# Squared lengths in 64-row tiles, and a new order of work between the two halves of a four-block network kernel

## The reference, cut to what matters

```python
# X is (8, 512, 128); every block is x = x + block(layernorm(x))
P = X @ W_in + b_in                      # 16 heads, each with Q, K, V, G of 64
d2 = q2[:, None] + k2[None, :] - 2*qk    # q2, k2: squared lengths of rows of Q, K
W  = (1e-4 + sqrt(max(d2, 0))) ** -2
W  = W / (1e-4 + sum(W, -1))
out1 = (G * (W @ V)) @ W_out + b_out
# block 2: 8 experts, top 2 of a softmax: sum_e r_e * (relu(x W1_e + b1_e) W2_e + b2_e)
# block 3: linear attention with decay;  block 4: 384 of 512 tokens go through gelu(x W)
```

## Time and profile before

| | us |
|---|---|
| median of 3 runs | 1470.9 (1470.77 to 1471.15) |
| the profiled execution | 1468.7 |
| its span, first to last instruction | 1466.6 |
| TensorE busy in the span | 1403.2 |
| ScalarE busy | 1098.1 |
| VectorE busy | 1059.6 |
| GpSimd busy | 851.9 |
| mean granted TensorE clock | 0.981 of 2.4 GHz |

### The profile page before, as it was taken

The page is one execution under the profiler, slowest core; times in us unless marked ns, Lnnn a source line. Parts: engine busy times, 40 slices in busy tenths (PEclk is TensorE's granted clock), DMA queues, the critical chain, the costliest instruction groups (busy, mean ns, idle before and its releaser), DMA issues.

```text
span 1466.6 us, 17689 instructions
## 1 busy us (share of the span) xinstructions
PE 1403.2 (96%) x6304; PEld 718.6 (49%) x6304; DVE 1059.6 (72%) x1944; ACT 1098.1 (75%) x943; POOL 851.9 (58%) x667
## 2 busy tenths in 40 slices
PE   6999999999999999999999999699999999999974
PEld 3433434434433443443444343256777777777753
DVE  6786777777777777777777677654677687786674
ACT  2799789879978978978878879845676676676741
POOL 4568767777777678768867876721333333333320
PEclk9999999999999999999999999899999999999985
DMA  3001111011001002001101103333011011010100
GB/s 114 0 16 23 30 30 24 15 45 23 16 16 51 16 16 51 16 17 30 37 16 30 30 16 96 89 123 103 0 66 58 8 66 55 11 66 8 59 7 8
DMA packets 45847, 55.09 MB, mean 38 GB/s; under 512 B 13825, under 2 KB 32513, under 8 KB 44609
## 3 DMA queue, kind: packets, MB, share of 16 engines
q1 hardware_dynamic: 45760, 53.97, 12.3%
HBM read 49.11 MB, written 4.85 MB: 37 GB/s over the span
## 4 chain that ended last, share of the span: by engine, by line
PE 89%; DVE 7%; POOL 1%; ACT 1%; issue 1%; DMA 0%; SPq 0%; DVEq 0%; POOLq 0%
PE sc L383 16%; PE av L396 14%; PE pj L74 13%; PE z L74 12%; PE y L1095 8%; PE sc L378 6%; PE y L74 5%; PE pj L362 4%; PE pj L412 4%; PE pj L404 2%; DVE w L541 2%; PE tb L1026 1%; POOL wsum L303 1%; PE tb L1040 1%; PE tb L1053 1%
## 5 line engine op out<-in xcount | busy, mean ns | idle before, releaser
L541 DVE TENSOR_SCALAR w<-sc 128x1024 f32<-128x1024 f32 x256 | 301.3, 1218 | 117.3 <-PE sc L383 115.2
L632 ACT ACTIVATE w<-w 128x2048 f32<-128x2048 f32 x128 | 237.5, 1904 | 144.5 <-DVE w L541 144.2
L303 POOL TENSOR_TENSOR wsum<-wsum,w 128x512 f32<-128x512 f32 x256 | 329.0, 1285 | 20.1
L882 POOL TENSOR_TENSOR hr_l<-hr,hr_h 128x512 fp32r<-128x512 f32 x112 | 150.2, 1341 | 265.0 <-ACT hr L928 265.0
L383 PE MATMUL sc<-query,key 64*128 64x512 f32 x1024 | 254.4, 615 | 0.0
L396 PE MATMUL av<-w,vt 128*64 128x512 f32 x1024 | 237.6, 607 | 6.4 <-DVE gT L548 5.2
L636 ACT ACTIVATE w<-w 128x2048 f32<-128x2048 f32 x128 | 240.2, 1901 | 0.4
L640 ACT ACTIVATE w<-w 128x2048 f32<-128x2048 f32 x128 | 239.6, 1895 | 0.0
L928 ACT ACTIVATE hr<-z,b 128x512 f32<-128x512 f32 x256 | 173.7, 684 | 77.3 <-PE z L74 77.2
L289 POOL TENSOR_TENSOR sqq<-query 128x512 f32<-128x512 f32 x64 | 66.5, 1040 | 223.0 <-DVE query L495 220.9
L300 POOL TENSOR_TENSOR wsum<-w 128x512 f32<-128x512 f32 x128 | 164.5, 1285 | 11.5 <-ACT w L640 11.5
(11 more groups left out here) (183 smaller groups left out, 2237.6 us busy)
## 6 DMA issues: line engine op xcount, KB each, us to landing
hT<-head_recips SPq DMA_DIRECT2D x64, 256.0 KB, 4.0
rb<-routing SPq DMA_DIRECT2D x8, 2048.0 KB, 7.0
w<-in_W SPq DMA_DIRECT2D x16, 256.0 KB, 5.0
xa<-in_X SPq DMA_DIRECT2D x8, 256.0 KB, 4.4
xc<-in_X SPq DMA_DIRECT2D x8, 256.0 KB, 2.8
x<-xc SPq DMA_DIRECT2D x8, 256.0 KB, 4.0
out<-prod SPq DMA_DIRECT2D x8, 256.0 KB, 2.3
x<-x SPq DMA_DIRECT2D x1, 1792.0 KB, 10.9
```

Of the source, the lines that this page charges most:

```text
L303: nc.gpsimd.tensor_tensor(wsum[:, u, :], wsum[:, u, :], w[:, j % 2, u, c, :], ALU.add).then_inc(s_added, 1)
L541: nc.vector.tensor_scalar(w[:, s, 2 * r:2 * r + 2, c, :], sc[:, i, :, :], 0.0, None, ALU.max).then_inc(s_d2, 1)
L632: nc.scalar.activation(w[:, j % 2, u, :, :], w[:, j % 2, u, :, :], ACT.Sqrt).then_inc(s_sqrt, 1)
```

## The change

1. **Rows in 64-row tiles.** `qrow` and `krow` hold head v of a pair at partitions 64v. `qrow` holds both pairs r of a quad in different rows of the same 64 (r = 0 at rows 0 to 3, r = 1 at rows 32 to 35), and `krow` gets one copy per pair, [P, 2, 2, T], which is zero in the other pair's rows. So L378 contracts over 64 rows, in the tiles of L383. The key rows take four VectorE instructions instead of two (`key_rows`: high and all, for r = 0 and 1, on one `high` tile), the query rows still two. `row_factors` in the prologue grows from 5 to 8 tiny instructions.
2. `nsel` and its load, and the tile `xn`, go: the layernorm writes in place, so `xa`'s next load waits for the transposes and stands after normalizer(j) of q = 2 instead of q = 1.
3. **Last quad's sums.** GpSimd no longer adds the chunks of quad 31; `last_sums` multiplies ones with all four chunks on TensorE, 16 fp32 products instead of 4.
4. **Order between the halves.** On all engines, as in the diff. ScalarE mixes the first relus among the last logarithms and powers; root_f(0) goes before the square roots.
5. Waits for the tail's loads, for `ones2`, for `w2s` and `x1_out` move to their first use.

```diff
-                        u = 2 * (g % 2) + v
-                        nc.tensor.matmul(sc[:, i, v, :], krow[32 * u:32 * u + 32, j % 2, c * P:(c + 1) * P],
-                                         qrow[32 * u:32 * u + 32, j % 2, :], start=True, stop=False)
+                        nc.tensor.matmul(sc[:, i, v, :], krow[halves[v], j % 2, g % 2, c * P:(c + 1) * P],
+                                         qrow[halves[v], j % 2, :], start=True, stop=False)
...
+            def last_sums():
+
+                n = bank(("sum", NQ - 1))
+                pe.wait_ge(s_w, 4 * NQ)
+                for c in range(NC):
+                    for u in range(4):
+                        m = nc.tensor.matmul(pj[32 * u:32 * u + 32, n, :], ones[:, :], w[:, (NQ - 1) % 2, u, c, :],
+                                             start=(c == 0), stop=(c == NC - 1))
                 m.then_inc(s_pj, 1)
...
+            def key_rows(j):
+                dve.wait_ge(s_pj_free, use["q2", j] + 1)
+                source = pj[:, bank(("k2", j)), :]
+                for r in range(2):
+                    if r == 1:
+                        dve.wait_ge(s_high, 4 * j + 3)
+                    high_rows(source, row_any[:, r, 1:2], row_one[:, r, 0:1])
+                    dve.wait_ge(s_high, 4 * j + 2 * r + 2)
+                    nc.vector.scalar_tensor_tensor(krow[:, j % 2, r, :], source, row[:, r, 3:4], high[:, :].bitcast(F32),
+                                                   ALU.mult, ALU.subtract).then_inc((s_high, s_pj_free)[r], 1)
...
-            sp.wait_ge(att["added"], 12 * NQ)
+            sp.wait_ge(att["pj"], use["sum", NQ - 1] + 1)
...
             square_roots, logarithm, power = att_scalar(act)
+            root_f(0)
             square_roots(NQ - 1)
-            root_f(0)
             nc.scalar.preload_act_table_set("natural_log_exp_and_others")
             logarithm(NQ - 1, 0)
-            for u in range(4):
-                if u < 3:
-                    logarithm(NQ - 1, u + 1)
-                if u == 3:
-                    exponential(0)
-                power(NQ - 1, u)
+            logarithm(NQ - 1, 1)
+            power(NQ - 1, 0)
+            power(NQ - 1, 1)
+            exponential(0)
+            logarithm(NQ - 1, 2)
             act.wait_ge(S["in_front"], 16 * len(front_loads))
+            hidden(0)
+            hidden(1)
+            power(NQ - 1, 2)
+            hidden(2)
+            hidden(3)
+            logarithm(NQ - 1, 3)
+            hidden(4)
+            power(NQ - 1, 3)
+            hidden(5)
+            turned_routing(0)
...
-                if (b, k) == (0, 0):
-                    sums(NQ - 1)
+                if (b, k) == (0, 1):
+                    turn_routing(0)
                 if (b, k) == (0, 2):
+                    weighted_values(NQ - 1, 1)
+                if (b, k) == (0, 3):
+                    last_sums()
+                if (b, k) == (0, 7):
                     output(NQ - 2)
-                if (b, k) == (0, 14):
+                if (b, k) == (0, 16):
                     output(NQ - 1)
-                if (b, k) == (0, 16):
+                if (b, k) == (0, 18):
                     turn_output(B - 1)
...
+            turn_f(0)
             pe.wait_ge(S["in_front"], 16 * len(front_loads))
-            turn_f(0)
             logits(0)
-            weighted_values(NQ - 1, 0)
-            weighted_values(NQ - 1, 1)
             for n in range(AHEAD):
                 if n == 2:
-                    turn_routing(0)
+                    weighted_values(NQ - 1, 0)
                 hidden(n)
...
-                if (b, k) == (0, 5):
+                if (b, k) == (0, 4):
+                    weighted_values(NQ - 1, 1)
                     sums(NQ - 1)
-                if (b, k) == (0, 6):
+                    for e in range(5, NE):
+                        split_w1(e)
+                if (b, k) == (0, 8):
                     output(NQ - 2)
-                if (b, k) == (0, 8):
                     dve.wait_ge(S["in_b2"], 16)
-                    dve.wait_ge(att["added"], 12 * NQ)
-                if (b, k) == (0, 9):
+                if (b, k) == (0, 12):
                     reciprocals(NQ - 1)
-                if (b, k) == (0, 19):
+                if (b, k) == (0, 20):
                     output(NQ - 1)
...
+            dve.wait_ge(att["added"], 12 * (NQ - 1))
+            front_norm(0)
             sums(NQ - 2)
             output(NQ - 3)
-            dve.wait_ge(att["added"], 12 * (NQ - 1))
-            front_norm(0)
-            split_w1(0)
             dve.wait_ge(S["turn_f"], 1)
             V.tensor_copy(xT_f[:, :], front_bank(0)).then_inc(S["xT_f"], 1)
             hand_over(0)
+            split_w1(0)
             dve.wait_ge(S["in_front"], 16 * len(front_loads))
             softmax_start(0)
-            reciprocals(NQ - 2)
-            for e in range(1, 4):
-                split_w1(e)
-            weighted_values(NQ - 1, 0)
+            split_w1(1)
             softmax_end(0)
             expert_ranks(0)
             routing(0)
-            for e in range(4, NE):
-                split_w1(e)
-            weighted_values(NQ - 1, 1)
+            weighted_values(NQ - 1, 0)
+            split_w1(2)
+            reciprocals(NQ - 2)
+            split_w1(3)
+            split_w1(4)
```

More of the change, by code:

```diff
@@ L110, in build_attention @@
         qrow = sb("qrow", [P, 2, T], F32R)
-        krow = sb("krow", [P, 2, T], F32R)
-        high = sb("high", [P, 2, T], F32R)
-        nsel = sb("nsel", [P, 2, P])
+        krow = sb("krow", [P, 2, 2, T], F32R)
+        high = sb("high", [P, T], F32R)
         head = sb("head", [P, 2, 32])
[L115 to L118, removed]
+        row = sb("row", [P, 2, 4])
+        row_one = sb("row_one", [P, 2, 2])
+        row_any = sb("row_any", [P, 2, 2])
+        both_one = sb("both_one", [P, 2])
+        both_any = sb("both_any", [P, 2])
+        row_low = sb("row_low", [P, 1])
         stats = sb("stats", [P, NC, 6])
@@ L244, in sync @@
             load_x(xc, 0, s_xc)
-            sp.wait_ge(s_xn, NC)
+            sp.wait_ge(s_pj, use["turn", 0, 1] + 1)
             load_x(xa, 1, s_xa)
@@ L271, in sync @@
                     load_x(xc, b, s_xc)
-                if q == 1 and b + 2 < B:
-                    sp.wait_ge(s_xn, NC * (b + 2))
+                if q == 2 and b + 2 < B:
+                    sp.wait_ge(s_pj, use["turn", b + 1, 1] + 1)
                     load_x(xa, b + 2, s_xa)
@@ L310, in normalize @@
                                         gT[:, 2 * q:2 * q + 2, :], ALU.mult).then_inc(s_hT, 1)
-            for j in PERIODS:
+            for j in range(-1, NQ):
                 if 0 <= j - 3 < NQ:
@@ L324, in gpsimd @@
                         add_chunks(j - 1, u)
+            return normalize
         def tensor(pe):
@@ L459, in tensor @@
                     step(j, k)
-            return weighted_values, sums, output, turn_output
+            return weighted_values, sums, last_sums, output, turn_output
         def vector(dve):
@@ L510, in row_factors @@
[L510 to L518, removed]
@@ L520, in high_rows @@
-            def high_rows(j, name):
-                h, out, factor, one, low = rows[name]
-                nc.vector.tensor_scalar(high[:, h, :], pj[:, bank((name, j)), :], factor, one,
-                                        ALU.mult, ALU.add).then_inc(s_high, 1)
-            def all_rows(j, name):
-                h, out, factor, one, low = rows[name]
-                dve.wait_ge(s_high, 2 * j + h + 1)
+                nc.vector.tensor_tensor(row_one[:, :, :], row[:, :, 0:4:2], row[:, :, 1:4:2], ALU.subtract).then_inc(s_row, 1)
@@ new lines, in row_factors, with high_rows, query_rows @@
+                nc.vector.tensor_scalar(row_low[:, :], row_low[:, :], 0.25, None, ALU.mult).then_inc(s_row, 1)
+                dve.wait_ge(s_row, 7)
+                nc.vector.tensor_scalar(both_any[:, :], both_any[:, :], 0.25, None, ALU.mult).then_inc(s_row, 1)
+                dve.wait_ge(s_row, 8)
+            def high_rows(source, factor, one):
+                nc.vector.tensor_scalar(high[:, :], source, factor, one, ALU.mult, ALU.add).then_inc(s_high, 1)
+            def query_rows(j):
+                if j >= 1:
+                    dve.wait_ge(s_pj_free, use["k2", j - 1] + 1)
+                source = pj[:, bank(("q2", j)), :]
+                high_rows(source, both_any[:, 0:1], both_one[:, 1:2])
+                dve.wait_ge(s_high, 4 * j + 1)
@@ L528, in all_rows @@
                 if j >= 2:
                     dve.wait_ge(s_sc, 8 * (j - 1))
-                nc.vector.scalar_tensor_tensor(out[:, j % 2, :], pj[:, use[name, j] % 3, :], low, high[:, h, :].bitcast(F32),
+                nc.vector.scalar_tensor_tensor(qrow[:, j % 2, :], source, row_low[:, 0:1], high[:, :].bitcast(F32),
                                                ALU.mult, ALU.subtract).then_inc(s_pj_free, 1)
+            def key_rows(j):
[8 more added lines that the diff above has]
```

(4 more changed lines are left out.)

56 lines of the change are left out of this document (30 added, 26 removed).

## The result

| | us |
|---|---|
| before, median of 4 runs beside it | 1471.0 |
| after, median of 4 runs | 1457.8 (1456.5 to 1458.3) |
| ratio, 95% interval | 0.991 (0.9895 to 0.9926) |
| profiled execution of after, its span | 1457.7, 1455.9 |

The kernel is 13.3 us faster. The forecast was 17.8 faster, 1453 us, with 1444 to 1465 around it. Step by step it can be compared only in the profiled executions, 1468.7 and 1457.7: there 17.8 were forecast and 11.0 came. The other 2.2 are no step of mine: the median before was 2.2 above its profiled execution, the one after is at its own.

A forecast was written before the change was run, and what follows sets the result against it. TensorE, busy 96% of the span, was taken to bound the first half, and its idle and slow time the seam. Terms -11.8 - 0.6 - 5.4 = -17.8 took 1468.7 to 1450.9, plus 2.2 for the median: 1453 us, range 1444 to 1465.

The forecast's parts named there:

- The gain per slot: First-half slots, L378 to L383: 64-row tiles in both steps save 0.20 us per slot, ends 0.10 and 0.24, 124 slots.
- Rival E: L378 to L383: the 0.20 belongs to the step from rows to heads whatever the tiles; 1478 us, chance 0.06.
- D: L378 to L383: half of the reconfiguration stays, saving 0.10 per slot; +12.4, 1465 us, chance 0.08.
- F: Row products: 64-row tiles run two side by side instead of four; +57, 1510 us, chance 0.01.
- The wait for krow: Ordinary quads, slot 0: TensorE waits 0.41 for the later key rows, starting 7.26 after slot 3; net -0.39 per quad.
- Rival C: Ordinary quads: no wait for krow, so 22 x 0.41 come back; 1444 us, chance 0.06.
- quad -1: +1.63; quad 0: +0.83: Start: longer krow waits before quad 0 and in its slot 3, less 0.20 saved per slot in quad 0.
- `nsel`: Prologue: dropping its 128 KB load brings TensorE's first product forward, -0.6 us, from 0 to -0.7.
- The seam: Between the halves: -7.2 us up to step 4, +1.8 later, sum -5.4, ends 0 and -9.
- rival B: Seam: relus among logarithms and exponentials need their own table loads, about 4 extra; 1458 us, chance 0.06.
- the late routing: Behind the seam: routing logits and exponential come late, so relu 23 delays hidden(25) in step 19; +1.8 us.
- Rival A: Seam gives nothing: relus obstruct TensorE as often as they free it, or late logits and output(31) cost 7; 1458 us, chance 0.14.

The follow-up runs named there:

- useless products: Changed kernel, with 11 and 12 products that nobody reads run on TensorE in the two long waits for key rows at the start: 1454.0 us, ratio 0.9892.
- the seam alone: Kernel before, with parts 2 to 5 of the change; rows stay in 32-row tiles with two key-row instructions: 1464.5 us, ratio 0.9963.
- part 3 alone: Kernel before, with GpSimd no longer adding the last quad's chunks and TensorE summing all four; all orders kept: 1465.3 us, ratio 0.9971.
- the rows alone: Kernel before, with parts 1 and 2 of the change; everything between the halves as before: 1461.5 us, ratio 0.994.

## Why the prediction was right, and where not

**The gain per slot: right in size, and partly by luck in its place.** 0.20 forecast, 0.197 measured by itself. I took all of it from the gap of 0.66 between L378 and L383, where two pairs at 0.23 would leave 0.20. The starts of the single products in the traces tell it otherwise. Before, the first pair of L378 is followed by the second after 0.34, by L383 after 0.32 more, and L383's second pair comes 0.53 behind its first. After, these are 0.34, 0.23 and 0.43. So a pair that follows a change of tile height comes about 0.10 late, and the next one again about 0.10. The step into the rows' tiles (from the 128-row tiles of L74) costs this in both kernels, and so does the step back to L74; the product ahead of L378 and the one behind L383 keep their distances. What went is one change of three per slot, from 32 to 64 rows: 0.09 ahead of L383 and 0.105 inside it. In my gap of 0.66, 0.10 belonged to the change before it, which stays, and I missed as much inside L383, which went. The two errors cancelled. The Trainium skill, "TensorEngine Tiling (Array Packing)", Tiling Modes, Key Properties, says that changing the tiling mode drains TensorE; it gives no figure. The trace agrees in that a change costs time, 0.20 us for the one that went. Rival E (the gap belongs to the step itself) falls with it, and so do D and F.

**The wait for krow: right.** 7.26 forecast and measured, net -0.39 per ordinary quad forecast and measured. Rival C fell. For q = 0 I had a wait of 0.10 at the fourth value; the quads lost 0.20 there (a wait and a slower start behind it), so that they gained 0.60 and not 0.70: 0.7 us in seven quads.

**The start: mis-sized, the largest error.** Forecast +1.9 behind the first product, measured +6.1. The step that failed is "quad -1: +1.63; quad 0: +0.83". It counted the two waits right and let the work behind them run at its old speed: a term put at nothing. The useless products showed 3.8 of the 4.2 too many as TensorE's clock. A row that should have warned stands in the earlier trace rows: the weighted values that took 5.74 after a pause, where the same 16 take 3.65 at the full clock (949.07 above). So did the kernel's first products before, which ran 0.43 apart behind their wait of 3.43 and 0.23 apart from 15.26 on. I used the low clock at the seam and not at the start.

**`nsel`: half its size.** -0.6 forecast, -0.35 in the two traces. (The loads up to there are eight, not the nine that I wrote.) In the ten traces the first product came at 11.31, 11.46 and 12.22 with the load, and at 10.89 to 11.12 (five) and 11.91 and 12.04 (two) without. So a load less is worth some 0.4, and chance in the loads' landing up to 1.

**The seam: mis-sized by 1.6.** -7.2 forecast to step 4, -5.65 measured. The splits, the relus without table loads (rival B fell) and the end of the gT wait came as written. The weighted values (31, 0) took 5.15 and not the 3.9 written down: the clock, granted 0.66 from 931 to 941, was low longer than I let it be. With the seam alone they took 3.87, so this part moves with the clock. The stretch of the late routing cost 2.1 where I had 1.8. Net the seam gave 3.5 and not 5.4. Rival A was wrong in its total but right in one half of its reason: on top of part 3 the mixed order gained nothing that could be measured. I credited the gain to parts 3 and 4 together; part 3 alone brings as much.

**The median.** I added the 2.2 that stood between the profiled execution and the median of before. After has no such distance. So 6.8 in the steps became 4.8 in the time: by luck, and not by a better reckoning.

## What to carry to other kernels

Before a wait is priced at its length, ask what clock the work behind it may run at: here two waits that grew by 1.6 each cost some 2 more each in slow products behind them. Two neighbouring matmul steps should have the same tile height where the operands allow it. What pays for it on another engine should be handed over in the pieces in which it is used: waiting for all key rows instead of the half that the next slot reads cost 9.3 us in the steady quads of the trace, and 12.7 by the medians, nearly what the whole change gave. When an engine is the late one at a seam, look who works beside it: taking GpSimd's adds away gave by itself as much as it gave together with a new order of five engines.

## What the runs showed of the hardware

- One change of tile height less per slot (128, 64, 128 rows in place of 128, 32, 64, 128) saved 0.197 us of TensorE's time, over 116 slots: about 0.09 before the first pair in the new tiles and 0.105 before the second. Four row products of 32 and of 64 rows otherwise take the same.
- TensorE's granted clock at the start was 1.00 (2.4 GHz) after a wait of 1.46 in the kernel before. After a wait of the same 1.46 in the kernel with the seam alone it was 0.66 over 24 to 29 us, so partly at the lower level (1.2 GHz), and L382 took 3.33. After the waits of 3.1 to 3.2 it was low both times in the kernel after (0.66, 0.53) and with the rows alone (0.50 over 24 to 29 us), but with the key rows made twice only after the first (0.66), and 1.00 after the second. Over the eight traces without useless products, two of the seven waits of 1.46 to 1.59 and eight of the nine of 3.1 to 3.2 were followed by slow products. What decides is open.
- With eleven products that nobody reads, 2.67 us of them in the wait, the clock stayed at 1.00, and the next step took 1.88 instead of 3.34. The products behind all four waits filled in this way, in two kernels, ran at full speed.
- A conversion and a subtraction on VectorE, 128x512, took 1.48 and 1.63 beside GpSimd's two-input adds and 0.42 and 0.69 without.
